# Layer 0's attention: products with v two steps late between the halves of the scores, items behind the second half

## What is computed

```
qkv = x @ W_attn + b_attn                      # 16 heads of 8, T = 1024
att = einsum('bhtd,bhsd->bhts', q, k) / sqrt(8)
att = att + alibi_causal_mask                  # slope_h * (s - t), -inf above the diagonal
att = softmax(att, axis=-1)
y   = einsum('bhts,bhsd->bhtd', att, v)
out = y @ W_proj + b_proj
```

## Time and profile before

| | |
|---|---|
| time, median of 3 runs | 576.47 us (573.36, 576.47, 579.17) |
| the profiled execution | 574.82 us, span 573.1 us |
| busy share of the span | PE 82%, DVE 65%, ACT 42%, POOL 34% |
| mean granted clock of PE | 0.936 |

### The profile page before, as it was taken

How to read it: one execution, slowest core, us unless ns; L and a number is a source line. 1 busy time by engine, 2 the same in 40 slices (tenths; PEclk the granted TensorE clock), 3 DMA queues, 4 the chain that set the end, 5 groups by cost and what they waited for, 6 DMA issues and landing times.

```text
span 573.1 us, 8339 instructions
## 1 busy us (share of the span) xinstructions
PE 471.3 (82%) x3004; PEld 192.8 (34%) x3004; DVE 371.3 (65%) x595; ACT 239.1 (42%) x460; POOL 193.9 (34%) x285
## 2 busy tenths in 40 slices
PE   7796787878787878878968767976899999989886
PEld 3262122222222222223326323633344433434342
DVE  5788687888888777762547788475178519752540
ACT  2574677777767777774650121111011111121120
POOL 3032425342222222221013625194018615871500
PEclk9997999999999999997968986798699999999999
DMA  6622512252020202000001310100013002300000
GB/s 211 220 72 54 159 63 100 63 188 63 3 63 2 64 2 63 2 3 3 0 2 55 146 56 18 57 37 0 1 62 105 37 0 74 121 9 1 19 1 18
DMA packets 19085, 31.78 MB, mean 55 GB/s; under 512 B 2544, under 2 KB 7120, under 8 KB 18724
## 3 DMA queue, kind: packets, MB, share of 16 engines
q1 hardware_dynamic: 19044, 31.24, 17.0%
HBM read 13.20 MB, written 8.06 MB: 37 GB/s over the span
## 4 chain that ended last, share of the span: by engine, by line
PE 61%; DVE 14%; ACT 10%; issue 6%; DMA 5%; SPq 4%; POOL 1%; ACTq 0%; DVEq 0%; POOLq 0%
PE PS L668 9%; ACT prob L1374 7%; PE PS L650 6%; PE PS L822 6%; PE PS L828 5%; PE PS L855 5%; PE PS L809 5%; PE PS L783 4%; DVE pmax L1064 4%; DMA k_op<-k_scr 3%; SPq L470 3%; PE PS L582 3%; PE PS L841 2%; PE PS L586 2%; DVE sm L1215 2%
## 5 line engine op out<-in xcount | busy, mean ns | idle before, releaser
L1064 DVE TENSOR_REDUCE pmax<-PS 128x8 f32<-128x1024 f32 x144 | 171.8, 1222 | 47.1 <-PE PS L582 31.7
L1374 ACT ACTIVATE prob<-PS 128x512 f32<-128x512 f32 (+1 forms) x320 | 159.9, 552 | 70.9 <-PE PS L650 67.8
L1514 POOL TENSOR_SCALAR_AFFINE_SELECT prob<-prob 128x512 f32<-128x512 f32 x64 | 39.9, 635 | 177.3 <-ACT prob L1374 177.3
L650 PE MATMUL PS<-q_op,k_op 55*128 55x512 bf16 (+3 forms) x384 | 60.9, 337 | 44.2 <-ACT prob L1374 41.8
L668 PE MATMUL PS<-prob,vaug 128*16 128x512 f32 (+3 forms) x768 | 82.4, 519 | 0.0
L1545 POOL TENSOR_TENSOR vdec<-vk,c_sb 128x256 f32<-128x256 f32 x56 | 34.6, 649 | 118.1 <-ACT vk L1398 118.1
L1441 ACT COPY oT<-PS 128x512 f32<-128x512 f32 x32 | 18.7, 585 | 122.6 <-PE PS L828 107.2
L582 PE MATMUL PS<-k_op,q_op 52*128 52x128 bf16 (+3 forms) x576 | 57.9, 277 | 8.5 <-DVE pmax L1064 5.4
L1215 DVE TENSOR_TENSOR sm<-PS,c_sb 128x512 f32<-128x512 f32 x64 | 41.2, 685 | 30.6 <-PE PS L809 30.4
L650 PEld LDWEIGHTS PS<-q_op,k_op 55*128 55x128 bf16 x384 | 18.4, 94 | 123.8 <-ACT prob L1374 110.3
L809 PE MATMUL PS<-qr,kr 64*128 64x512 f32 x128 | 38.7, 684 | 18.6 <-DVE sm L1215 15.5
(11 more groups left out here) (178 smaller groups left out, 510.9 us busy)
## 6 DMA issues: line engine op xcount, KB each, us to landing
turned<-by_sin SPq DMA_DIRECT2D x80, 128.0 KB, 2.0
k_op<-k_scr SPq DMA_DIRECT2D x14, 220.0 KB
q_op<-q_scr SPq DMA_DIRECT2D x14, 208.0 KB
c_sb<-const_dram SPq DMA_DIRECT2D x1, 2576.0 KB, 8.5
q_scr<-part_a SPq DMA_DIRECT2D x6, 256.0 KB, 3.4
k_scr<-part_a SPq DMA_DIRECT2D x6, 256.0 KB, 3.6
q_scr<-part_b SPq DMA_DIRECT2D x6, 256.0 KB, 3.4
k_scr<-part_b SPq DMA_DIRECT2D x6, 256.0 KB, 3.9
```

Of the source, the lines that this page charges most:

```text
L650: last = mm(PS[:, (GH * s + h) % ST_BANKS, at:at + nn], k_op[rows, slot, h // 2, P * j:P * j + P], q_op[rows, slot, h // 2, P * i0:P * i0 ...
L1064: vec.tensor_reduce(pmax[:, of_pair, at:at + step * (TPS - 1) + 1:step], both.rearrange("p a (b c) -> p a b c", c=P), AX.X, ALU.max).then_ ...
L1374: sca.activation(prob[:, s % P_SLOTS, h, 0:UNIT_W[u]], PS[:, k % ST_BANKS, 0:UNIT_W[u]], ACT.Exp).then_inc(s_exp, 1)
```

## The change

Products with v are taken two steps late instead of one (`PV_LAG` = 2), and stand between the two halves of the scores. All items of a step stand behind the second half. ACT follows: the copy to `yacc` moves between the two pairs of exponentials, two steps late; its items move behind all four exponentials. DVE, POOL and SP are as before.

```diff
-P_SLOTS = 3
+P_SLOTS, PV_LAG = 3, 2
@@ PE
-            for s in range(NSTEP + 1):
-                beside = items_of_step(s) if s < NSTEP else ()
-                for half in range(2):
-                    if s < NSTEP:
-                        scores(s, range(GH // 2 * half, GH // 2 * (half + 1)))
-                    for k in (beside[:len(beside) // 2], beside[len(beside) // 2:])[half]:
-                        item(k)
-                if s:
-                    pv(s - 1)
+            for s in range(NSTEP + PV_LAG):
+                if s < NSTEP:
+                    scores(s, range(GH // 2))
+                if s >= PV_LAG:
+                    pv(s - PV_LAG)
+                if s < NSTEP:
+                    scores(s, range(GH // 2, GH))
+                for k in items_of_step(s) if s < NSTEP else ():
+                    item(k)
@@ ACT
-            for s in range(NSTEP + 1):
+            for s in range(NSTEP + PV_LAG):
                 u = s % NU
-                beside = items_of_step(s) if s < NSTEP else ()
...
-                    for k in (beside[:len(beside) // 2], beside[len(beside) // 2:])[half]:
-                        item(k)
-                if s:
-                    acc(s - 1)
+                    if half == 0 and s >= PV_LAG:
+                        acc(s - PV_LAG)
+                for k in items_of_step(s) if s < NSTEP else ():
+                    item(k)
```

## The result

Before 574.55 us (median of 20 runs), after 577.42 (20 runs, 573.20 to 579.25). Run by run beside each other on the same chips the ratio is 1.0066, 95% interval 1.0045 to 1.0086: 3.8 us slower (2.6 to 4.9); the two medians differ by 2.9. That is a real loss, and a small one: under the 1% that I had called about what can be told from no change. I had forecast +10.5, 587.0.

A forecast was written before the change was run, and what follows sets the result against it. Two chains of copies and DMAs, not the ring, were taken to set each ten-step period. Groups +6.5, start +1.4, steps 63 to 79 -2.8 and clock +5.4 gave +10.5: 587 us, own range 581 to 593, wide 574 to 595.

The forecast's parts named there:

- the term of steps 63 to 79: Layer 0's last attention steps, no loads following: gains in the ring and transpose steps, less some losses, -2.8 us.
- The term of the clock: New PE wait before the scores of u=3 brings a half-clock stretch: 0.9 in each of six groups, +5.4 us.
- The two chains through DMAs: In each ten steps (four heads), copies of maxima feed DMAs; later copies lengthen six groups, +6.5 us together.
- the loop: Both DMA chains and the stretches between them, one group's period: 28.59 us before, 29.70 forecast.
- the ring: Order of scores, products and exponentials within a step: 2.46 us against 2.78, gain 0.3 where DVE keeps up.
- chain (a): Copy of maxima at u=5 (place in ten steps), small DMAs, four loads, item of u=9: 10.18 us; PE waits 1.0.
- Rival 2: The loads do not bind: sum of groups about +2, total 577 us; chance 0.12.
- rival 3: The ring decides if SP's chains have room: 0.3 in eight of ten steps, total 560 us; chance 0.12.
- copy (b): Copy of maxima at u=1, 7.33 after the item (was 6.74); S0 (first scores half) of u=3 follows 4.44 later.
- the start: Steps 0 and 1, five items each, DVE sets their time; first items start later: +1.4 us, bounds 0 and 2.
- copy (a): Copy of maxima at u=5, forecast 7.75 us after the first scores half of u=3 instead of 6.82: +0.93.
- rival 1: The loop lengthens but the clock holds: +5.1, total 581.6 us; chance 0.25.

The follow-up runs named there:

- e7: Kernel before, with the new order only from step 63 on; ratio 0.9870 to the kernel before.
- e11: e5 with the turns of steps 5 to 65 behind the second half, their copies behind all four exponentials; ratio 1.0097 to the kernel before.
- e5: Kernel before with only the products moved, items left in two halves; ratio 0.9894 to the kernel before.
- e1: Changed kernel, SP issuing the four operand loads ahead of the first half's four small DMAs; ratio 0.9968 to the kernel before.
- e9: Changed kernel with extra unread matmuls filling PE's waits for DMAs at u=3 and u=9; ratio 1.0142 to the kernel before.
- e4: Kernel before, SP issuing the four operand loads ahead of the first half's four small DMAs; ratio 0.9950 to the kernel before.
- e10: Kernel before with the new order from step 63 and the loads issued ahead of the small DMAs; 562.72 us, ratio 0.9817.
- e8: Changed kernel with the new order only until step 62, the old one from step 63; ratio 1.0148 to the kernel before.
- e2: Changed kernel with the turns of steps 5 to 65 taken back between the halves; ratio 0.9950 to the kernel before.

## Why the prediction was wrong in size, step by step

The step that failed is the term of steps 63 to 79: I had -2.8 and it is -7.0 in the traces, -7.5 (5.2 to 9.6 gained) by e7. It was the one term to which I gave no bounds. The term of the clock, +5.4, was too large as well; what lengthens the groups was right.

**Right: what bounds the groups.** The two chains through DMAs, and the late copies that lengthen them. For the loop without a fall of the clock I had 7.75 + 10.18 + 7.33 + 4.44 = 29.70; the group shown is 7.86 + 10.87 + 7.21 + 4.44 = 30.38, and that from step 23 29.88. Only the loads were longer than I took (10.3 to 10.9 in all four groups that wait for them). The group with the extra items: 31.9 forecast, 31.96. Steps of u=6 and 7 came 2.52 apart, 2.75 before: the ring's gain is there, and is given back at the next wait. The waits named appeared: k_op at u=9 in four groups (1.17 to 1.94; I had five at about 1), q_op at S0 of u=3 in all seven (0.67 to 2.35). e11 against e5 shows that the copies do it, e1 that chain (a) is a part. Rival 2 (loads do not bind) fell, and so did rival 3: its gain would have needed copy (b) to S0 in under 1, and that stayed at 4.44 in six of the seven (4.62 ahead of step 13).

**Nearly right: the start.** +2.0 in the trace, 1.4 forecast. S0 of step 3 starts at 66.1 and 65.1 in two more traces with the start of the changed kernel (e1, e9), and at 63.3 to 64.1 in three with the old one (e4, e7, e10).

**Wrong: the term of steps 63 to 79.** -2.8 forecast, -7.0 in the traces, -7.5 by e7. Part by part, between the first exponentials: steps 66 to 68 -0.8 (0.9 forecast), 71 to 74 -2.6 (13.08 to 10.47; 2.55 forecast), 76 -0.5 (0.2). So the ring and, in their sum, the transposes were sized well. Their parts were not: step 71 gave 0.87, as my own 3.5 and 2.65 have it, and not the 1.2 in my sum, while 72, 73 and 74 gave 0.68, 0.62 and 0.44 where I had 0.5, 0.5 and 0.35. That these come to 2.6 is luck. What I missed: step 78, narrow and with transposes like the others, gave 1.0 more (3.61 to 2.56), and I had left it out; 69 and 70 gave 0.7, where I had nothing; the 0.8 that I charged for the square root and for products at low clock didn't come (from the first exponential of step 75 to the last yacc copy the time fell from 22.83 to 21.42). And steps 63 to 65 gave 1.5 (9.61 to 8.09): the half-clock stretch of the earlier trace rows, which I had read as what the change would bring about and not as something that it could also take away. In e4, of the old order, that stretch falls in steps 71 to 74 instead (14.54 against 13.08) and the tail is as long. By the clock column the old order's tail has 19 to 20 us at 0.50 (63.87 x 0.15 x 2 in before, e4 likewise), the new one 17 in after, 14 in e7 and 7 in e10, which is also the shortest (54.56). So three things failed: I costed only the steps whose rows I had looked at, guessed losses, and counted the clock on one side only.

**Too large: the clock.** I charged 0.9 in each of six groups, +5.4. In after the clock fell in three of the six (0.93, 0.90 and 0.94; the others hold 1.00). What it cost there can be read against the group shown, which has no low stretch and takes 7.86 and 7.21. S0 to copy (a) took 8.35 from step 3 (66.16 to 74.51), 9.14 from step 13 (95.13 to 104.27) and 8.39 from step 53 (219.96 to 228.35), and item to copy (b) took 8.11 in the group from step 13 (115.19 to 123.30): 0.5 + 1.3 + 0.5 + 0.9 = 3.2. Against that the loads took 10.92, 10.37, 10.87 and 10.26 where I had 10.18, 1.7 in all. Together 6.5 + 3.2 + 1.7 = 11.4. The traces have 11.3, and 6.5 + 5.4 = 11.9 was forecast: near by two errors that make up for each other.

Timed, start and groups cost less than that. I had 7.9 without the clock and 13.3 with it, and the two traces have 13.3. e8 gives 8.5 (5.6 to 11.4), and the direct ratio with e7's tail gives 3.8 + 7.5 = 11.3. Part of the difference is chance of the one execution of before that is profiled: against the 175.2 of e7, of the same order, after's six groups are +8.9 and not +11.3. By how much the clock's term and the loop's are too large over many executions isn't settled; the loop without the clock (6.5 + 1.4) already accounts for e8.

**The sum.** 8.5 - 7.5 = +1.0 from e7 and e8, +3.8 measured directly; both within the other's error. Forecast +10.5: 4 to 5 of the 6.7 too much is the tail, the other 2 lie in start and groups. A further 1.9 of the miss of 587 lies in its footing, the median of three runs (576.47), where 20 runs have 574.55. The time is the one I gave for rival 2 (577), but not for its reason: the loads do bind. It is rival 1's loop with a tail that gives more. The direction was right and 577.42 lies in the wide range of 574 to 595, not in the forecast's own of 581 to 593; I gave 0.55 to slower by over 1%, and it came out within 1%.

## What to carry to other kernels

When work is reordered on an engine, look at what a DMA waits for: a copy that feeds a chain of DMAs belongs as early as its inputs allow, and here it cost 2% to put two of them per ten steps behind two more exponentials. The same edit can gain where no such chain follows: split it by stage (here from step 63 on), and look first at whether independent DMAs can go ahead of the waiting ones on their queue. When you add up a stretch, go through every step of it, not those whose rows are at hand, and count the clock as a gain too where pauses go away.

## What the runs showed of the hardware

- A pause of PE and the clock. In after, S0 of u=3 waited 2.12, 2.35, 0.67, 0.67, 1.58, 2.16 and 2.17 us; each of the four waits over 2 in the groups from steps 3, 13, 53 and 63 goes with a stretch of 3.4 us at 0.50 within 1.6 us of its end (from 67.5, 94.8, 221.1 and 251.8), and none of the three shorter ones does. PE was busy 2.28 of the last 4.44 us before S0(53). In e1 the waits of 2.64, 2.12 and 2.13 have one too, those of 0.62, 0.63 and 1.52 none. (Its first, of 1.05, ends inside a stretch that began at 49.8.) It is not the wait alone: in e2 the one of 1.69 that ends at 65.33 has a stretch from 65.4, and of the k_op waits in after that of 1.94 has one and that of 1.91 has none.
- What such a stretch costs. Step 13 of after took 3.53 instead of 2.46, step 3 2.94, step 53 3.00, step 63 2.69: 0.2 to 1.1 each in the step, 0.5 to 1.3 by the loops above. The Trainium skill, "TensorE: Matmul & The Clock Gate", section "HAM oscillation — how this bites in real kernels", describes waits for DMAs that put the clock to half rate each time round; the traces agree that such waits do it, but not each time round: before S0 of u=3 in four of the seven groups of after. Filling the waits with extra work held the clock at 1.00 for 119 us in e9, and that kernel was slower (1.0142 against 1.0066).
- What the 4.44 is made of. In the chain of after the four small DMAs behind copy (b) at 215.52 are issued by SP at 216.10, 216.82, 217.52 and 218.20, 0.64 to 0.67 us each for the first three, and the last has landed 1.7 us after its issue; the scores start at 219.96. So 2.1 of this wait are SP's issuing of the first three, one behind the other, and 1.7 the last one's way. Nothing here tried to issue them from elsewhere or as fewer.
- The order of issue on SP. Behind four small DMAs that wait for copy (a), the four loads are in use 10.0 to 11.0 us after the copy, wherever PE waits for them in before, after, e5 and e11. Putting them ahead of those DMAs gave 1% to the changed kernel and 0.5% to the one before.
